# Three units of a set turned in blocks as one group, with GpSimd issuing its own mask loads

## The reference

```python
x = _layernorm(x + _L0_gnn_ref(x, adj, ...))   # adj @ x, message, GRU cell
x = _layernorm(x + _L1_gnn_ref(x, adj, ...))   # normalised adj @ (x @ weight) + bias
x = _layernorm(x + _L2_gnn_ref(x, adj, ...))   # 4-head attention, masked by adj == 0
x = _layernorm(x + _L3_gnn_ref(x, adj, ...))   # hyperbolic layer, adj @ xt
# the attention layer:
attn = jnp.einsum('nhc,mhc->hnm', q, k) / np.float32(np.sqrt(C))
neg = jnp.where(adj == 0.0, -jnp.inf, attn);  m = max(neg);  e = exp(neg - m)   # 0 where masked
out = jnp.einsum('hnm,mhc->hnc', e / sum(e), v)
# then, per row: a gate beta = sigmoid([out, x_r, out - x_r] @ Wb), the blend, the layer norm (x3),
# and for the last layer mx = x3 @ weight.T and a chain of norms, artanh, tanh (Moebius product and sum) to xt
```

## Time and profile before

| | us |
|---|---|
| median of three runs | 1786.12 |
| profiled execution | 1782.96 |
| its span | 1781.3 |
| outside the span | 1.66 |
| attention, first transposes to last attended unit | 578.4 to 1539.2 |

### The profile page before, as it was taken

The page is one execution under the profiler, slowest core; times in us unless marked ns, Lnnn a source line. Parts: engine busy times, 40 slices in busy tenths (PEclk is TensorE's granted clock), DMA queues, the critical chain, the costliest instruction groups (busy, mean ns, idle before and its releaser), DMA issues.

```text
span 1781.3 us, 40266 instructions
## 1 busy us (share of the span) xinstructions
PE 1735.9 (97%) x15000; PEld 1131.3 (64%) x15000; DVE 1228.6 (69%) x2405; ACT 975.8 (55%) x1505; POOL 895.6 (50%) x849
## 2 busy tenths in 40 slices
PE   7999999999998999999999999999999999999996
PEld 3444444444444778877877887778778777644442
DVE  4777775222225889999999999999999999301322
ACT  0110111010103898999999999999999999411101
POOL 0212120112114755778878788788787896540211
PEclk9999999999998999999999999999999999999998
DMA  9866676899996544445445445454454543897981
GB/s 382 325 221 251 254 252 224 278 313 371 332 366 184 186 155 161 155 155 167 150 140 182 150 152 170 156 173 150 142 178 144 167 157 116 323 371 275 321 323 57
DMA packets 134029, 388.53 MB, mean 218 GB/s; under 512 B 15712, under 2 KB 66144, under 8 KB 109280
## 3 DMA queue, kind: packets, MB, share of 16 engines
q1 hardware_dynamic: 117792, 356.11, 57.6%
q10 hardware_dynamic: 13824, 22.75, 3.6%
q0 software_dynamic: 2240, 7.34, 1.6%
HBM read 333.19 MB, written 52.95 MB: 217 GB/s over the span
## 4 chain that ended last, share of the span: by engine, by line
PE 92%; DVE 4%; issue 1%; ACT 1%; DMA 1%; POOL 1%; DVEq 0%; ACTq 0%; POOLq 0%; SPq 0%
PE bank L592 35%; PE bank L742 23%; PE bank L763 14%; PE bank L701 13%; DVE arena L1281 2%; PE bank L580 1%; PE bank L655 1%; PE bank L614 1%; PE bank L613 1%; DMA arena<-x_dram 1%; PE bank L607 0%; PE bank L769 0%; PE bank L650 0%; PE bank L789 0%; PE bank L630 0%
## 5 line engine op out<-in xcount | busy, mean ns | idle before, releaser
L976 ACT ACTIVATE arena<-arena,small 128x2048 f32<-128x2048 f32 x256 | 516.2, 2016 | 2.8 <-DVE small L1281 2.8
L742 PE MATMUL bank<-ident,arena 128*128 128x128 f32 x3592 | 485.5, 278 | 4.4 <-ACT arena L976 2.6
L742 PEld LDWEIGHTS bank<-ident,arena 128*128 128x128 f32 x3592 | 398.1, 141 | 87.8 <-issue 41.9
L592 PE MATMUL bank<-arena,stat_s 128*128 128x512 f32 x1008 | 439.1, 592 | 2.1 <-issue 1.2
L988 ACT ACTIVATE arena<-bank 128x512 f32<-128x512 f32 x673 | 377.0, 604 | 66.2 <-PE bank L742 65.3
L701 PE MATMUL bank<-k,parts 128*128 128x512 f32 x1024 | 354.4, 436 | 10.6 <-DVE small L1281 10.6
L592 PEld LDWEIGHTS bank<-arena,stat_s 128*128 128x128 f32 x1008 | 189.2, 190 | 226.8 <-issue 225.4
L763 PE MATMUL bank<-arena,stat_x 128*32 128x128 f32 x8192 | 276.5, 276 | 0.0
L763 PEld LDWEIGHTS bank<-arena,stat_x 128*32 128x32 f32 x8192 | 208.1, 109 | 90.8 <-issue 81.5
L592 PE MATMUL bank<-arena,stat_x 128*128 128x512 f32 x512 | 228.3, 598 | 10.1 <-DMA arena<-adj_cols 7.8
L701 PEld LDWEIGHTS bank<-k,parts 128*128 128x128 f32 x1024 | 158.8, 192 | 29.6 <-DVE small L1281 24.5
(11 more groups left out here) (155 smaller groups left out, 1431.8 us busy)
## 6 DMA issues: line engine op xcount, KB each, us to landing
arena<-adj_cols SPq DMA_DIRECT2D x190, 1024.0 KB, 6.4
stat_s<-adj SPq DMA_DIRECT2D x85, 512.0 KB, 4.8
group_dram<-stat_s SPq DMA_DIRECT2D x63, 512.0 KB, 2.9
arena<-group_dram SPq DMA_DIRECT2D x252, 128.0 KB, 2.8
arena<-adj SPq DMA_DIRECT2D x43, 512.0 KB, 4.6
parts<-q_dram SPq DMA_DIRECT2D x128, 64.0 KB, 2.4
k<-k_dram POOLq DMA_DIRECT2D x28, 256.0 KB, 9.5
x_dram<-arena ACTq DMA_DIRECT2D x16, 256.0 KB, 3.7
```

Source lines behind the costliest of these rows:

```text
L592: mm_ = pe.matmul(bank[:, to, :], stat[:, jt, :], ring[:, s, j, :], start=(jt == 0), stop=(jt == TILES - 1))
L742: last = pe.transpose(bank[:, b_, h * P:(h + 1) * P], cols[:, st % SETS, h, u * P:(u + 1) * P], ident[:, :])
L976: act.activation(cols[:, s_, h, :], cols[:, s_, h, :], ACT.Exp, bias=shift[:, t % 2, 1, i:i + 1], scale=-1.0, accum_out=blocksum[:, t % 2, ...
```

## The change

1. `BLOCK_TURN_AT` turns three units of a set in blocks (13, 14, 15, at places 1, 2, 6) instead of two, stored and fetched as one group of three; PE turns 13 of 16.
2. The group has slots of its own in `spilled`, so its load waits for the group before and no longer for a unit's buffer; `turned` is counted by `slot_of`.
3. PE attends in batches of 4, 6 and 6 units at places 4, 8 and 14 instead of four batches of 4.
4. The lists of who copies (`BY_VECTOR` 23 units, `BY_SCALAR` 81) and the exponents' places are new; `norm_h` moves from 113 to 115 and the logarithms from 119 to 121.
5. The mask buffers go from three to two. From the seventh mask on GpSimd issues the load itself, behind the bias that frees the buffer and a wait on that bias's own semaphore. SP keeps the first six and everything else; `store_xt` now stands behind `load_group`.
6. `SPILLED` grows from four chunks to six (0 to 5); the product of layer 3 waits for all of them before its first slot, and `load_xt` waits also for the last group's use.

```diff
-ATTEND_BATCH = 4
-ATTEND_LAG = 8
-BLOCK_TURN_AT = {14: 3, 15: 5}
-GROUPS = ((14, 15),)
+ATTENDS = {4: (-4, -3, -2, -1), 8: (0, 1, 2, 3, 4, 5), 14: (6, 7, 8, 9, 10, 11)}
+BLOCK_TURN_AT = {13: 1, 14: 2, 15: 6}
+GROUPS = ((13, 14, 15),)
...
-MASK_AHEAD = 8
-MASKS = 3
-SPILLED = (2, 3, 4, 5)
+FIRST_MASKS = 6
+MASKS = 2
+SPILLED = (0, 1, 2, 3, 4, 5)
...
+def slot_of(k):
+
+    return (PE_UNITS + LAST_UNITS).index(k) % TURNED
...
-                if g * UPS + GROUPS[i][-1] >= TURNED:
-                    sp.wait_ge(unit_used, g * UPS + GROUPS[i][-1] - TURNED + 1)
+                if g > 0:
+                    sp.wait_ge(unit_used, (g - 1) * UPS + GROUPS[i][-1] + 1)
...
                     g = c * SPC + st
-                    load_mask_ahead(c, 2 * st + 0)
                     if g < GROUP_SETS:
                         store_group(g, 0)
+                    if g < GROUP_SETS:
+                        load_group(g, 0)
                     if st == 0 and c - 2 in SPILLED:
                         store_xt(c - 2)
-                    if g < GROUP_SETS:
-                        load_group(g, 0)
...
-                    load_mask_ahead(c, 2 * st + 1)
...
+                sp.wait_ge(unit_used, GROUP_SETS * UPS)
                 for i in range(len(SPILLED)):
...
-                    if (k - ATTEND_LAG) % ATTEND_BATCH == 0:
-                        for a in range(k - ATTEND_LAG, k - ATTEND_LAG + ATTEND_BATCH):
-                            if a >= 0:
-                                attend(c, a, first)
-                            elif not first:
-                                attend(c - 1, UPC + a, False)
+                    for a in attended_at(c, k):
+                        if a >= 0:
+                            attend(c, a, first)
+                        elif not first:
+                            attend(c - 1, UPC + a, False)
...
+            pe.wait_ge(xt_in_place, 16 * len(SPILLED))
...
                 g = c * COLS + m
-                pool.wait_ge(adj_landed[g % MASKS], 16 * (g // MASKS + 1))
+                if g < FIRST_MASKS:
+                    pool.wait_ge(adj_landed[g % MASKS], 16 * (g // MASKS + 1))
+                else:
+                    pool.wait_ge(mask_landed[g % MASKS], 16 * ((g - FIRST_MASKS) // MASKS + 1))
                 pool.nop(nofuse=True)
                 pool.tensor_scalar(maskbias[m % 4], adj_in[g % MASKS], 0.0, MASKED, ALU.is_equal,
                                    ALU.mult).then_inc(bias_ready, 1)
+                after = g + MASKS
+                if FIRST_MASKS <= after < CHUNKS * COLS:
+                    pool.wait_ge(bias_ready, g + 1)
+                    row = after // BLOCKS * P
+                    col = after % BLOCKS * BLOCK
+                    pool.dma_start(adj_in[g % MASKS], adj[row:row + P, col:col + BLOCK]
+                                   ).then_inc(mask_landed[g % MASKS], 16)
```

More of the change, by code:

```diff
@@ L198, in last_bank_before, with attended_at, used_before @@
     return TURN_BANKS.uses[LAST_USE + 1 + LAST_UNITS.index(k) - len(TURN_BANKS.BANKS)][1]
+def attended_at(c, k):
+    u = k % UPS
+    return [k - u + a for a in ATTENDS.get(u, ())]
+def slot_of(k):
+    return (PE_UNITS + LAST_UNITS).index(k) % TURNED
+def used_before(c, k):
+    i = (PE_UNITS + LAST_UNITS).index(k) - TURNED
+    return c * UPC + PE_UNITS[i] + 1 if i >= 0 else (c - 1) * UPC + PE_UNITS[i] + 1
 BY_VECTOR = [k for k in PE_UNITS if (k % 16 in VECTOR_PLACES or k in VECTOR_ALSO) and k not in VECTOR_NOT]
@@ L287, in build_program @@
         cols = arena[:, 0:RING].rearrange("p (s h n) -> p s h n", s=2, h=H)
+        spilled = stat_s[:, SPILLED[0] * TPC:(SPILLED[-1] + 1) * TPC, :].rearrange("p t f -> p (t f)")
         turned = [stages[i] for i in (0, 1, 6, 7, 2, 3, 10, 11)]
[L289 to L293, removed]
+        adj_in = (arena[:, RING + 4 * CHUNK:RING + 6 * CHUNK], spilled[:, 0:2 * CHUNK])
+        group_slots = spilled[:, 2 * CHUNK:5 * CHUNK]
+        blocks = [stat_s[:, TILES - 3 * TPC:TILES, :].rearrange("p t f -> p (t f)")]
         maskbias = [half_[:, i * BLOCK:(i + 1) * BLOCK] for half_ in
@@ L305, in slots_of @@
         def slots_of(i):
-            first, n = GROUPS[i][0] % TURNED - 6, len(GROUPS[i])
-            return group_slots[:, first * CHUNK:(first + n) * CHUNK]
+            return group_slots[:, 0:len(GROUPS[i]) * CHUNK]
         def tiles(ap):
@@ L347, in build_program @@
         adj_landed = [sem(f"adj_landed{s}") for s in range(MASKS)]
+        mask_landed = [sem(f"mask_landed{s}") for s in range(MASKS)]
         q4_landed = [sem(f"q4_landed{s}") for s in range(2)]
@@ L541, in _ @@
                              q_parts[:, i, :].bitcast(F32)).then_inc(gcn_q_out, 16)
-            load_mask(0, 5)
+            load_mask(0, 4)
             sp.wait_ge(gcn_dve, CV(last, "root"))
             sp.dma_start(root_dram[:, last * CHUNK:CHUNKS * CHUNK], root_out).then_inc(gcn_root_out, 16)
-            for m in range(6, MASK_AHEAD):
+            for m in range(5, FIRST_MASKS):
                 load_mask(0, m)
@@ L815, in attention @@
                 if last_chunk:
-                    for a in range(UPC - ATTEND_LAG, UPC):
+                    for a in range(UPC - 4, UPC):
                         attend(c, a, first)
@@ L849, in _ @@
             HELD_BANKS = (0, 4, 5)
-            product(2, 0, {0: [final_out], SPILLED[0] - 1: [lambda: pe.wait_ge(xt_in_place, 16 * len(SPILLED))], 5: [lambda: pe.wait_ge(att_pool, AG(last - 1, "xt"))],
+            pe.wait_ge(xt_in_place, 16 * len(SPILLED))
+            product(2, 0, {0: [final_out], 5: [lambda: pe.wait_ge(att_pool, AG(last - 1, "xt"))],
                            6: [lambda: turn_x3(last, 2)]}, slots=range(SLOTS - 1))
@@ L1049, in attention @@
                         block_weights(c, k // UPT)
[L1050 removed]
+                    if k in BY_SCALAR or (last_chunk and k in LAST_BY_SCALAR):
                         copy_unit(c, k, first)
@@ L1377, in attention @@
             def attention(c, first, last_chunk):
-                post = post_steps(c - 1, 107 if last_chunk else 113) if not first else {}
+                post = post_steps(c - 1, 107 if last_chunk else 115) if not first else {}
                 for k in range(UPC):
```

62 lines of the change are left out of this document (27 added, 35 removed).

## The result

The changed kernel takes 1864.88 us (median of 4 runs, 1862.31 to 1867.76), the kernel before 1785.83 on the same chip: a ratio of 1.044 [1.042, 1.046]. It is slower, as forecast, but by 79 us and not by 40, and outside the range, which ended at 1850.

The account below looks back on a forecast made before the run. It took PE's pace and an equally long GpSimd-then-DVE chain as the bounds; -4 + 42.8 - 1.3 - 1.2 + 3.5 = +39.8 on the profiled 1782.96 gave 1822.8, as a median 1826 us, range 1785 to 1850.

Parts of the forecast that it names:

- What bounds the kernel: Attention loop: PE sets the pace; equally long, GpSimd's 84.78 us from xn to y plus DVE's 35.08, together 119.86.
- So an issue is 0.55 + 0.08 = 0.63 us: GpSimd between xn and y: each of 11 mask issues costs 0.63 us (bounds 0 and 0.98), making 84.78 into 91.7.
- The 1.3 us taken off for two masks without an issue: Six attention loops: 1.3 us subtracted from +42.8 because two masks at the end have no issue.
- The clock term: After PE's stop in each loop: half speed costs 2.4 us of PE work, of which 1.2 reaches the loop.
- DVE's gain itself: From y to xn, DVE's 36 places at 0.9125 instead of 0.936: 0.85 less, minus 0.1 slack, giving 34.1 us.
- The group of three. Hidden: Group's round trip: store and load, 9.6 us, fit in some 12.7 us; otherwise PE waits 1 or 2 us per set.
- the predicted -4 for the faster pace: From 578 to the first xn: 11 sets in steady pace, each 0.38 us shorter, give -4 us.
- PE waits 3.5: Layer 3 start: six xt tiles needed, the last landing at 1542.8, so PE waits 3.5 us; bounds 0 and 5.
- The 1.2 us of faster pace: After the last xn: 51 places, each 0.0235 us shorter, give -1.2 us.
- The free issue: Rival: GpSimd's mask issue costs 0 us, loop 118.9, sum -7.7, median 1778; chance 0.16.
- Late masks: Rival: masks land 9.5 us from issue, about 3.2 us more per loop, +19, 1845; chance 0.10. Forecast took 0.
- DVE's kept waits: Rival: DVE keeps its waits at 15.26 us per set, +18 over 63 sets, 1808 if issues are hidden; chance 0.07.

Follow-up runs that it names:

- number 5: Kernel before, plus a small unused 128x4 GpSimd operation and a wait for it behind each mask bias, SyncE still issuing every mask: 1813.34 us.
- number 7: Kernel before with GpSimd issuing mask loads into three buffers, each issue put one bias later: 1834.38 us.
- number 1: Kernel before with only the mask issue moved: GpSimd issues loads behind the bias from the seventh mask, three buffers, groups of two: 1858.94 us.
- number 6: Kernel before, plus an unused 128x4 power on GpSimd and a wait for it behind each mask bias, SyncE still issuing every mask: 1873.07 us.
- number 9: Changed kernel with each GpSimd mask load cut to an eighth of its size (64 KB in place of 512 KB): 1854.03 us.
- number 3: Changed kernel without any mask load after the first six, output not the reference's: 1779.92 us.
- number 4: Changed kernel with layer 3's product waiting for one xt tile ahead of each slot instead of all six before the first: 1858.95 us.
- number 10: Changed kernel with the group's store and loads cut to a twelfth of their bytes, masks as they are: 1852.35 us.
- number 8: Changed kernel (two mask buffers) with each GpSimd mask issue put one bias later: 1998.67 us.

## Why the prediction was wrong, step by step

**What bounds the kernel: right.** GpSimd's chain to `stats` and DVE's way to the next `bias_mx` make up the loop one behind the other. Four kernels that put time on GpSimd in the kernel before lie near one line: numbers 5, 7, 1 and 6 added 0.36, 0.65, 0.92 and 1.15 us per mask (number 1 without its last loop) and lost 29.4, 50.4, 73.5 and 89.1 us, 1.16 to 1.25 us for each us of 66 masks (number 1 with the stall told below), although two of them move issues and two move nothing.

**"So an issue is 0.55 + 0.08 = 0.63 us": the step that failed.** The mechanism was right and the term too small: an issue cost 0.92, near the upper bound of 0.98: 0.30 for the wait and 0.62 for the issue. The stretch to `stats` grew by 10.0 us in the mean of the first five loops instead of 6.9, some 18 us in six. The 1.3 us taken off for two masks without an issue didn't come: the last issue (1556.6) lies behind the last loop's `stats` (1536.28), so all six loops have eleven. Number 7 took the wait away and was left with 0.65. The prediction took the wait from a dependent small step, 0.16 us behind its source. The rows it needed stood in its own group: the earlier trace rows has two mask biases that waited 0.25, one behind a 128x512 step and one behind a small one, against the 0.16 of one small step behind another. And the 0.554 was the median of loads of another shape; 0.819 was the longest of them. The Trainium skill's page "DMA: Bandwidth & Descriptors", section "Anatomy of one DMA — SWDGE (gpsimd) path", puts the sequencer's dispatch at about 50 ns and calls descriptor generation small. The trace shows an issue in one piece and not these parts; the whole took 0.61 to 0.62 us for 512 KB and 0.60 to 0.61 for 64 KB (number 9), so the 0.05 per issue that the prediction worked out from the page is excluded. The measurement decides.

**The clock term: right in kind, small.** PE stood idle for 7.45 us and the clock was 0.50 (1.2 GHz) when it resumed, 0.71 in the mean of the window from 1144 to 1148, and 1.00 in the next. The prediction let 1.2 us of it reach the loop. Against number 3, where no such stop occurs, the stretch from `stats` to `bias_mx` is 2.0 us longer (35.29 to 33.31): 0.8 more per loop, 5 us. The group's late transfers aren't the cause: in number 9, where they are all but gone, the stretch is 35.32. That the clock is, numbers 5 and 7 show: the stretch took 35.68 to 35.75 us in all six of their loops in which the clock was at 0.57 to 0.60 behind `stats`, and 34.13 to 34.16 in five of the other six. DVE's gain itself (0.85, with the slack of 0.1) is confirmed by number 3: 34.33 to 33.31.

**One stall of 3.0 us** in the sixth loop was in no step. It is the same in the changed kernel and in numbers 1, 4, 9 and 10 (that loop's stretch to `stats` is 2.6 to 2.8 us longer than the rest), each time ahead of the 114th of the 122 issues, and the profile names no releaser:

```profile
1490.77 3.65 POOL L1556 TENSOR_SCALAR arena<-stat_s 128x1024 bf16<-128x1024 f32 x1 [0.25 <-POOL small L1690]
1497.44 0.65 POOL L1563 DMA_DIRECT2D stat_s<-adj  x1 [3.02 <-issue]
```

**"The group of three. Hidden": failed, in the first chunk above all.** The prediction set 9.6 us for a store and a load against a room of 12.7, by landing times of single transfers. The trace shows the whole trip. SyncE, then PE's row behind it:

```profile
744.08 0.34 SPq L462 DMA_DIRECT2D group_dram<-stat_s  x1
749.18 1.74 SPq L473 DMA_DIRECT2D stat_s<-group_dram  x4
```

```profile
757.90 0.86 PE L771 MATMUL bank<-stat_s,stat_x 128*32 128x128 f32 x24 [1.36 <-DMA stat_s<-group_dram]
```

From the store at 744.08 to PE's start are 13.8 us: 5.1 until the load can be issued, 1.7 to issue its four parts, and 7 for the last of them to land beside a mask. The prediction's own fallback, 1 or 2 us per set, was the right size, and in the loops it costs nothing because PE waits for GpSimd's chain anyway. Ahead of the first `bias_mx` no such cover exists: there numbers 9 and 10, which take away the masks' bytes or the group's, both reach 771.2, 4.7 us under the kernel before. Part of this is scatter, since their attention starts 3.4 and 3.7 us earlier than the changed kernel's. Free of it are the eleven sets from the second set's block turn on DVE (604.37) to the thirteenth's (771.50): 167.13 us after, 163.95 before, and 159.4 in numbers 3, 9 and 10 alike. So the predicted -4 for the faster pace was right (-4.6), and 7.7 us of collision of the two transfers were missing; between 557 and 784 us PE waited 7.2 us for the group, in six places. Neither transfer does it alone. Number 1, with groups of two and GpSimd's mask loads, took 165.91, 2.0 more than the kernel before, and its PE waited 1.7 us for groups there; so some of it comes without the group of three.

**"PE waits 3.5" for layer 3: too small.** PE's first product, beside the earlier trace rows:

```profile
1606.17 4.50 SPq L507 DMA_DIRECT2D stat_s<-xt_dram  x6
...
1622.32 6.28 PE L601 MATMUL bank<-arena,stat_s 128*128 128x512 f32 x8 [6.37 <-issue]
```

PE was free at 1615.95, 9.8 us behind the issue, where it had been 11.1; the tiles land up to 13.7 us behind theirs. The idle time brings the granted clock down to 0.80 and 0.78 in the two windows of 8 us from 1616 on, and the first slot takes 6.28 instead of 3.70. The 6.37 lie outside the prediction's bounds of 0 and 5; SyncE issued the tiles 35.1 us behind the seventh `bias_mx`, where it had been 33.0, the delay that the upper bound had in view. The slot's 2.6 were in no step. The 1.2 us of faster pace didn't come: PE was free 44.85 us behind the seventh `bias_mx`, before 44.2. So 6.4 + 2.6 + 0.6 = 9.6 us, of which 0.9 came off further behind; measured are 8.8.

**Rivals.** The free issue is excluded by numbers 1 and 9, and number 5 shows that GpSimd has no room for one. Late masks: in the six loops of the changed kernel one bias waited for its mask, for 0.9 us, so a landing term of 0 was right. DVE's kept waits: excluded by number 3, whose loop (118.42) needs the faster pace.

Together, of the 45 us that were missing between the profiled executions: the issue's size is 18 to 19, the part up to the first `bias_mx` 11.5 (7.7 of collision and 3.5 ahead of the attention, which is scatter and no step's fault), layer 3 6.5, the clock's and the stall's share 7, the masks without an issue 1.3.

## What to carry to other kernels

An instruction that only issues a DMA isn't counted as busy and still takes its place in the engine's order: before moving one, ask not how busy the engine is but whether its chain sets an end, and add to the issue the wait ahead of it, with the largest wait of this kind that the rows show as its bound. And when two traces are compared stage by stage, start from a mark behind the stages in which nothing changed: here 3.5 us had come from ahead of it. A transfer that is hidden by three microseconds when each half is taken at its average is not hidden beside the one that the same change starts; look at the stretch where nothing else covers it. And a buffer given up (three masks to two) takes away the freedom to reorder: it made the one cheap repair of the issue's wait, number 8, the slowest kernel of all.

## What the runs showed of the hardware

- GpSimd's DMA issue takes 0.60 to 0.62 us whatever it moves (medians, 512 and 64 KB), and waiting for its own mask bias before it 0.30 us on top; SyncE issued a mask in 0.43 us (median, kernel before).
- PE idle for 7.45 us (1135.80 to 1143.25) came back at a clock of 0.50 and had 1.00 in the window from 1148 on; the stretch that follows was 2.0 us longer, in the mean of six loops, than where there was no such stop (number 3). In number 5 the loops with a clock of 0.57 behind the stop took 1.6 us more than those with 1.00.
- A single stall of 3.0 us ahead of the 114th of the 122 issues, at the same place in five kernels (the changed one, numbers 1, 4, 9 and 10) and absent in number 7. Its cause wasn't looked for further and stays open.
